# Attention scores of a Macaron layer: queries and keys split in two float32r parts instead of three bf16 parts

## The reference

```python
x = x + 0.5 * ffn(layernorm(x))      # 8 experts, top 1 by a router, 128 -> 512 -> 128
x = x + attention(layernorm(x))
x = x + 0.5 * ffn(layernorm(x))
# attention: 16 heads of DK = 8, 1024 tokens
q = (x @ Wq + bq); k = (x @ Wk + bk); v = (x @ Wv + bv)
scores = einsum('bhsd,bhtd->bhst', q, k) / sqrt(8)
ctx = einsum('bhst,bhtd->bhsd', softmax(scores), v)
return ctx @ Wo + bo
```

## Time and profile before

| what | value |
|---|---|
| time, 3 runs | 999.62 us median, 999.19 to 999.98 |
| span of the profiled execution, first to last instruction | 996.9 us |
| what lies around the span, by the median | 2.7 us |
| PE busy | 907.5 us (91%) |
| DVE busy | 832.2 us (83%) |
| ACT busy | 750.2 us (75%) |
| POOL busy | 219.1 us (22%) |
| mean granted PE clock | 0.963 of full speed |

### The profile page before, as it was taken

How to read it: one execution, slowest core, us unless ns; L and a number is a source line. 1 busy time by engine, 2 the same in 40 slices (tenths; PEclk the granted TensorE clock), 3 DMA queues, 4 the chain that set the end, 5 groups by cost and what they waited for, 6 DMA issues and landing times. The chain is left out here.

```text
span 996.9 us, 18005 instructions
## 1 busy us (share of the span) xinstructions
PE 907.5 (91%) x5949; PEld 385.6 (39%) x6023; DVE 832.2 (83%) x1404; ACT 750.2 (75%) x1507; POOL 219.1 (22%) x317
## 2 busy tenths in 40 slices
PE   5799927899999999999999999999999999965996
PEld 4699923322222222222222222222222222434996
DVE  6776628989999999999999999999999998768664
ACT  4367706978888888888888888888888888754774
POOL 3168841831000000000000100000100000024775
PEclk9989957999999999999999999999999999996998
DMA  7632135752220213202022120220202000051311
GB/s 262 194 96 73 41 116 190 238 192 63 58 61 16 62 34 81 62 17 62 15 73 74 31 62 15 73 54 28 75 30 64 29 23 17 2 169 48 105 63 44
DMA packets 65443, 75.14 MB, mean 75 GB/s; under 512 B 12896, under 2 KB 43784, under 8 KB 65352
## 3 DMA queue, kind: packets, MB, share of 16 engines
q1 hardware_dynamic: 58776, 60.98, 20.6%
q0 software_dynamic: 5120, 12.59, 4.1%
q10 hardware_dynamic: 1456, 0.41, 0.2%
HBM read 40.47 MB, written 33.49 MB: 74 GB/s over the span
## 5 line engine op out<-in xcount | busy, mean ns | idle before, releaser
L1574 DVE TENSOR_REDUCE maxima<-ps_m 128x2 f32<-128x1024 f32 x512 | 602.8, 1221 | 53.8 <-PE ps_m L1335 52.8
L1544 ACT ACTIVATE probs<-ps_s 128x512 f32<-128x512 f32 x1024 | 555.9, 600 | 109.5 <-PE ps_s L1381 77.7
L1381 PE MATMUL ps_s<-q,k 74*128 74x512 bf16 (+1 forms) x950 | 294.5, 385 | 3.0 <-ACT probs L1544 0.9
L1392 PE MATMUL ps_o<-probs,vs 128*32 128x512 f32 x2048 | 272.7, 605 | 0.7 <-ACT probs L1544 0.7
L1381 PEld LDWEIGHTS ps_s<-q,k 74*128 74x128 bf16 (+1 forms) x1024 | 79.5, 97 | 303.4 <-ACT probs L1544 217.1
L1335 PE MATMUL ps_m<-k,q 64*128 64x512 bf16 x1024 | 159.9, 385 | 13.8 <-ACT probs L1544 7.9
L1265 POOL TENSOR_SCALAR split<-top 128x16 bf16<-128x16 f32 x32 | 8.1, 253 | 445.8 <-DVE top L1590 428.7
L1335 PEld LDWEIGHTS ps_m<-k,q 64*128 64x128 bf16 x1024 | 49.1, 93 | 102.7 <-issue 58.1
L693 PE MATMUL ps_y<-W,hT 128*128 x624 | 83.8, 278 | 0.0
L1392 PEld LDWEIGHTS ps_o<-probs,vs 128*32 128x32 f32 x2048 | 40.3, 108 | 109.3 <-issue 95.1
L693 PEld LDWEIGHTS ps_y<-W,hT 128*128 128x128 f32 x624 | 77.0, 194 | 0.6 <-issue 0.4
(11 more groups left out here) (215 smaller groups left out, 586.3 us busy)
## 6 DMA issues: line engine op xcount, KB each, us to landing
k_rows<-parts SPq DMA_DIRECT2D x24, 384.0 KB, 4.5
sums<-oT SPq DMA_DIRECT2D x30, 256.0 KB, 3.6
q<-q_parts SPq DMA_DIRECT2D x75, 96.0 KB
k<-k_rows SPq DMA_DIRECT2D x15, 288.0 KB
token_rows<-x SPq DMA_DIRECT2D x16, 256.0 KB, 4.1
token_rows<-v_and_ctx SPq DMA_DIRECT2D x16, 256.0 KB, 3.6
k<-k_rows SPq DMA_DIRECT2D x15, 256.0 KB
q_parts<-parts SPq DMA_DIRECT2D x8, 384.0 KB, 3.4
```

Of the source, the lines that this page charges most:

```text
L1381: nc.tensor.matmul(ps_s[n % 3][:, :], k2[buffer(g)][0:contracted, j, kt * P:(kt + 1) * P], q2[buffer(g)][0:contracted, j, u * HALF:(u + 1) ...
L1392: last = nc.tensor.matmul(ps_o[32 * j:32 * (j + 1), :], vs[buffer(g)][:, kt, j, :], probs[:, s % 2, j, :], start=(kt == 0), stop=(kt == KT ...
L1544: nc.scalar.activation(probs[:, s % 2, j, :], ps_s[n % 3][:, :], ACT.Exp, scale=SCALE).then_inc(exped, 1)
L1574: nc.vector.tensor_reduce(maxima[:, :, pr, qt, kh], ps_m[slot][:, :, :], AX.X, ALU.max).then_inc(unit_free[slot], 1)
```

## The change

Parts are now float32r numbers, two for each value (PARTS = 2), with 2 x 2 x 8 = 32 rows of products. They, three repeated key pieces (AGAIN = 3, 24 rows, beside queries that are zero), six rows of ones beside zeros, and the two guards fill rows 0 to 63 for even heads and rows 64 to 127 for odd heads. A max unit contracts 62 rows, a score product 64, and odd and even heads lie in different halves of the rows. `second_part` and `third_part` are gone: the remainder is the second part. Stores send each part once; the load repeats it. The number of buffers of `parts` (SPLITS) goes from 3 to 2. The two max units of a step no longer stand together. The fills are whole tiles, 9 in all, and stand in the first FFN's front, before the gathers.

```diff
-PARTS = 3
+PARTS = 2
 ROWS = PARTS * PARTS * DK
-MAX_ROWS = ROWS - DK
+ODD = P // 2
 GUARDS = 2
-SCORED = ROWS + GUARDS
+AGAIN = 3
+GUARD = ODD - GUARDS
+SCORED = GUARD + GUARDS
...
-    FILLED = 4 * BUFS
+    PIECES = 3
+    FILLED = PIECES * BUFS
...
         if piece == 0:
-            self.nc.gpsimd.memset(self.k2[p][64:96, 0::2, :].bitcast(F32), self.PAIR).then_inc(self.filled, 1)
+            self.nc.gpsimd.memset(self.k2[p][:, :, :].bitcast(F32), 1.0).then_inc(self.filled, 1)
...
+        pool.wait_ge(self.normed_pool, len(self.BY_POOL))
+        for n in range(self.setup.FILLED):
+            self.setup.gpsimd_fill(pool, n)
         pool.wait_ge(self.route.stored, 2 * 16 * QUADS)
...
         for t in range(TILES):
             scatter(t)
-            if self.setup and t < self.setup.FILLED:
-                self.setup.gpsimd_fill(pool, t)
...
-SPLITS = 3
+SPLITS = 2
...
-        parts = sb("parts", [P, SPLITS, 2, PARTS, HALF], BF16)
+        parts = sb("parts", [P, SPLITS, 2, PARTS, HALF], F32)
...
-        LOADS, STORES = 2 * PARTS + 1 + 3, 1 + PARTS
+        LOADS, STORES = 2 * PARTS + 2 * PARTS * PARTS + 2 * AGAIN, 2
...
+                for n in range(PARTS):
+                    for m in range(PARTS):
+                        row = product(j, n) + m * DK
+                        engine.dma_start(k[row:row + DK, :, tokens].bitcast(F32), k_rows[n, :, :, :]).then_inc(landed, 16)
+                for n in range(AGAIN):
+                    row = j * ODD + ROWS + n * DK
+                    engine.dma_start(k[row:row + DK, :, tokens].bitcast(F32), k_rows[n % PARTS, :, :, :]).then_inc(landed, 16)
...
-                store_key(sp, QUADS - 3, 0)
                 place_guard(0)
-                store_rest(QUADS - 3)
-                for q in range(QUADS - 2, QUADS):
+                for q in range(QUADS - 3, QUADS):
                     store(q)
...
-                    for j in (2 * pr, 2 * pr + 1):
-                        rows = slice(j % 2 * MAX_ROWS, (j % 2 + 1) * MAX_ROWS)
-                        last = nc.tensor.matmul(ps_m[slot][:, j % 2, :], q2[buffer(g)][rows, j, qt * P:(qt + 1) * P],
-                                                k2[buffer(g)][rows, j, kh * HALF:(kh + 1) * HALF], start=True, stop=True)
+                    for j in range(2):
+                        rows = slice(j * ODD, j * ODD + GUARD)
+                        last = nc.tensor.matmul(ps_m[slot][:, j, :], q2[buffer(g)][rows, pr, qt * P:(qt + 1) * P],
+                                                k2[buffer(g)][rows, pr, kh * HALF:(kh + 1) * HALF], start=True, stop=True)
...
-                    nc.tensor.matmul(ps_s[n % 3][:, :], k2[buffer(g)][0:contracted, j, kt * P:(kt + 1) * P],
-                                     q2[buffer(g)][0:contracted, j, u * HALF:(u + 1) * HALF], start=True, stop=True).then_inc(scored, 1)
+                    nc.tensor.matmul(ps_s[n % 3][:, :], k2[buffer(g)][rows, j // 2, kt * P:(kt + 1) * P],
+                                     q2[buffer(g)][rows, j // 2, u * HALF:(u + 1) * HALF], start=True, stop=True).then_inc(scored, 1)
...
-                    for unit in units:
+                    for unit in units[:1]:
                         do_unit(*unit)
-                    for j in range(GH - 1):
+                    for j in range(2):
                         score(g, k, j)
+                    for unit in units[1:]:
+                        do_unit(*unit)
+                    score(g, k, 2)
                     if s:
                         values(s - 1)
                     score(g, k, GH - 1)
...
-                    nc.scalar.activation(parts[:, q % SPLITS, j, 1, :], rem[:, q % 2, j, :], ACT.Copy).then_inc(middle, 1)
...
-                for j in range(2):
-                    third_part(dve, nc.vector, LAST, j)
```

More of the change, by code:

```diff
@@ L6 @@
 BF16 = mybir.dt.bfloat16
+F32R = mybir.dt.float32r
 I32 = mybir.dt.int32
@@ L982, in attention @@
         top, negated = (sb(name, [P, 2, GH // 2 * QUAD], F32) for name in ("top", "negated"))
-        split = sb("split", [P, 2, GUARDS, GH // 2 * QUAD], BF16)
-        blocks = [sb(f"blocks{p}", [P, 4 * KT], BF16) for p in range(2)]
+        split = sb("split", [P, 2, GUARDS, GH // 2 * QUAD], F32)
+        blocks = [sb(f"blocks{p}", [P, 4 * KT], F32) for p in range(2)]
         ps_m = [ctx.enter_context(nc.psum_tensor(f"ps_m{p}", [P, 2, HALF], F32)) for p in range(2)]
@@ L1012, in use, with product @@
             return g // BUFS
-        def product(j, n, m=0):
-            row = (n * PARTS + m) * DK
-            return row if j == 0 else MAX_ROWS + row if row < MAX_ROWS else row - MAX_ROWS
-        def guard(j):
-            return ROWS if j == 0 else DK
+        def product(j, n):
+            return j % 2 * ODD + n * PARTS * DK
         def load_queries(engine, g, landed, tokens=slice(0, SEQ)):
@@ L1036, in load_keys @@
             for j in range(2):
-                k_rows = dram["k_rows"][b, :, :, :, slice(first + j, first + GH, 2), tokens].rearrange("n m d i t -> (n m d) i t")
-                many = ROWS if j == 0 else MAX_ROWS
-                engine.dma_start(k[product(j, 0):product(j, 0) + many, j::2, tokens], k_rows[0:many, :, :]).then_inc(landed, 16)
-            engine.dma_start(k[0:DK, 1::2, tokens], k_rows[MAX_ROWS:, :, :]).then_inc(landed, 16)
+                k_rows = dram["k_parts"][b, :, :, slice(first + j, first + GH, 2), tokens]
+                for n in range(PARTS):
[5 more added lines that the diff above has]
+                    engine.dma_start(k[row:row + DK, :, tokens].bitcast(F32), k_rows[n % PARTS, :, :, :]).then_inc(landed, 16)
         def high_parts(q):
@@ L1074, in stores_landed, with parts_done @@
                 engine.wait_ge(query_stored, 16 * (q + 1))
[L1076 removed]
+        def parts_done(engine, q, count):
             if q == LAST:
[L1079 removed]
+                engine.wait_ge(left[0], 2 + count)
             else:
[L1081 removed]
+                engine.wait_ge(left[min(q, FIRST)], 2 * max(q - FIRST, 0) + count)
         def landed_results(q):
@@ L1146, in place_guard @@
                     for j in range(2):
-                        sp.dma_start(q2[buffer(g)][guard(j):guard(j) + GUARDS, j::2, u * HALF:(u + 1) * HALF], rows[j, :, :, :]).then_inc(in_m[buffer(g)], 16)
+                        sp.dma_start(q2[buffer(g)][j * ODD + GUARD:j * ODD + SCORED, :, u * HALF:(u + 1) * HALF].bitcast(F32), rows[j, :, :, :]).then_inc(in_m[buffer(g)], 16)
                 def results(g, u):
@@ L1432, in _ @@
                 pe.wait_ge(high, high_parts(QUADS))
-                parts_done(pe, left, LAST, 2)
+                parts_done(pe, LAST, 2)
                 pe.wait_ge(v_out, QUADS)
@@ L1491, in high_part @@
                         nc.scalar.activation(exact[:, q % 2, j, :], bank[:, :], ACT.Identity, bias=bias[:, 0:1]).then_inc(high, 1)
-                    nc.scalar.activation(parts[:, q % SPLITS, j, 0, :], bank[:, :], ACT.Identity, bias=bias[:, 0:1]).then_inc(high, 1)
+                    nc.scalar.activation(parts[:, q % SPLITS, j, 0, :].bitcast(F32R), bank[:, :], ACT.Identity, bias=bias[:, 0:1]).then_inc(high, 1)
                 def high_both(q):
-                    parts_done(act, left, q - 2, 2)
+                    parts_done(act, q - 2, 2)
                     if q >= SPLITS:
@@ L1532, in _ @@
                         normalise(q + 2)
-                    for j in range(2):
-                        second_part(q, j)
-                parts_done(act, low, LAST - 1, 2)
-                parts_done(act, low, LAST, 2)
+                parts_done(act, LAST - 1, 2)
                 for s in range(SOFT):
@@ L1684, in remainder @@
                     dve.wait_ge(high, high_parts(q) + j + 1)
-                    nc.vector.scalar_tensor_tensor(out=rem[:, q % 2, j, :], in0=bank[:, :], scalar=bias[:, 0:1], in1=parts[:, q % SPLITS, j, 0, :],
-                                                   op0=ALU.add, op1=ALU.subtract).then_inc(left[q % LAST], 1)
+                    nc.vector.scalar_tensor_tensor(out=parts[:, q % SPLITS, j, 1, :].bitcast(F32R), in0=bank[:, :], scalar=bias[:, 0:1],
+                                                   in1=parts[:, q % SPLITS, j, 0, :], op0=ALU.add, op1=ALU.subtract).then_inc(left[q % LAST], 1)
                 front.vector(dve)
@@ L1769, in layer @@
         }
-        q2, k2 = ([sb(f"{n}{p}", [P, GH, SEQ], BF16) for p in range(BUFS)] for n in ("q2_", "k2_"))
+        q2, k2 = ([sb(f"{n}{p}", [P, GH // 2, SEQ], F32R) for p in range(BUFS)] for n in ("q2_", "k2_"))
         vs = [sb(f"vs{p}", [P, KT, GH, 32], F32) for p in range(BUFS)]
```

80 lines of the change are left out of this document (22 added, 58 removed).

## The result

The changed kernel is slower: 1065.2 us median of 4 runs (1061.18 to 1075.87) against 999.8 beside it, a ratio of 1.067 (95%: 1.063 to 1.071). The forecast was 956, the range 926 to 1002. The profiled execution has a span of 1059.1, 62.2 more than before.

A forecast was written before the change was run, and what follows sets the result against it. PE was taken to bound the loop (2.62 us a step) and POOL the first FFN's end. Against a median of 999.62, fills -10.1, step -34, last steps -1.5 and attention's start +2.5 made -43, so 956 us; range 926 to 1002.

The forecast's parts named there:

- Loop's transfers: Loop, SP's loads: 18 issues instead of 10 stay hidden; if not, 0 to 5 us in all.
- It adds 0 ... I take the bf16 end: Loop, float32r weight load behind the values, once a step: adds 0 as bf16; 0.10 (+25 us) as f32, for the range.
- the fills: First FFN, POOL: fills no longer behind the scatters, -10.1 us; at their new place they cost 0.
- one slot for a float32r product and halves that overlap: Loop, PE: float32r streams 512 columns in one slot and halves overlap, so PE needs 1.97 to 2.2 us a step.
- rivals 1 and 2: Loop, PE: float32r halves don't overlap (about 1044, chance 0.06); a float32r product streams twice or more (1045 to 1145, chance 0.08).
- the two floors of 2.40: Loop step: DVE's work and the chain through ACT's exponential each need 2.40 us, against 2.62 before.
- the allowance of 0.08: Loop step: 0.08 us added to 2.40 for unit B's wait and ACT's copy of ps_o, giving 2.48, -34 us.
- The start of attention: Before the loop: parts drop out, 2.5 us gained; waiting for quad 5's stores costs 5; net +2.5, between -4 and +7.
- Rival 3: Loop: weight load, drains between halves or unit B's wait leave a step of 2.58 to 2.63, 981 to 998; chance 0.20.
- Rival 4: Loop: PE's granted clock falls; +265 us if at 1.2 GHz throughout, +27 for a tenth of the steps; chance 0.04.
- The last 11 steps: End of the loop: scores 0 and 1 overlap in the six steps with a "y" unit, -1.5 us.

The follow-up runs named there:

- e12: The changed kernel with AGAIN = 0, so without the repeated key pieces and with 12 transfers a load: 996.71 us, ratio 0.996.
- e5: The changed kernel without copies, with bf16 parts in place of float32r and three buffers of parts: 949.18 us, ratio 0.949.
- e10: The changed kernel's layout with three bf16 parts, seven of nine products, two guards, 8 transfers a load, no copies, fills first: 948.25 us, ratio 0.946.
- e11: The kernel before with one change, its own 12 fills ahead of the gathers in the first FFN: 990.13 us, ratio 0.992.
- e8: The changed kernel without copies, with quad 5's stores issued ahead of the first guards: 991.36 us, ratio 0.991.
- e9: The changed kernel once more, nothing altered, for a comparison on one chip: 1065.61 us, ratio 1.068.
- e4: The kernel before with its 12 fills ahead of the gathers, the same kernel as e11 on another chip: 1051.91 us, ratio 0.999.
- e3: The changed kernel with 12 key transfers of each load writing 16 partitions of one head instead of 8 of two: 1181.05 us, ratio 1.122.

## Why the prediction was wrong

**The step that failed: "Loop's transfers. ... Hidden; if not, a few tenths 16 times, 0 to 5 us."** It cost 60 us in the loop, and about 4 more at the attention's start. The prediction counted how long SP issues (7 us where it was 4), and compared the guards' transpose at step 5 with their use at step 8. It named SP's wait for the results behind the load but gave it no length. They land when the load has drained: with the 18 transfers that takes 17.5 us at the place shown, with the 10 of before 8.8 (498.03 to 506.82), with e12's 12 11.7. The chain is load, results, guards, max unit, and its slack is SP's idle time before `guards<-blocks`, 4.2 us in the kernel before (3.2 to 4.4 over the groups). The earlier trace rows end where the answer begins: SP's wait behind the load, and how fast a load drains, weren't read. Most late guards were then paid twice: by PE's wait (41.4 us in all 13), and by work at the granted clock 0.50 behind it; the steps that follow the 13 waits are 12.5 us longer together than their 2.67.

**"It adds 0 ... I take the bf16 end": mis-sized.** The float32r weight load takes 185 to 193 ns, near f32's 194, and adds to the chain twice in a step, not once: at score 3 behind the values, and at score 2, which waits for ACT. The step of the kernel without copies is 2.617 on average; with bf16 it is 2.45, against 2.48 predicted. In us: first to last values 673.8 (e12) against 630.2 (e5) and 630.3 (e10), so this term is +43.5, where the bound was +25. This alone turns a gain of 40 us in the loop (35 predicted) into a loss of 3. The Trainium skill, TensorE: Matmul & The Clock Gate, section Weight-path perf modes, has fast weight load only where the weights aren't FP32. The trace bears it out if float32r counts as FP32: 185 ns in e12, 94 in bf16.

**Right: the fills** (-10.1 by e11, -10.1 predicted), on a chip where POOL ends last (in the profiles with the changed kernel's own fills x is loaded 8.1 to 10.1 us sooner); **one slot for a float32r product and halves that overlap**, so rivals 1 and 2 fell; **the two floors of 2.40**: bf16 in the same layout makes 2.39. That its average, 2.45, is so near the predicted 2.48 is in part luck: the allowance of 0.08 was for unit B's wait and ACT's copy of `ps_o`, and what fills it in e5 is PE's wait for the guards, 10.0 us, more than its 4.5 for DVE.

**The start of attention**: +4.3 against +2.5, the mechanism as predicted in part. ACT waited for quad 5's stores (3.09 us; 4.97 in e12), and putting them first is worth 5.4 us (e8). The longer wait, 5.68 us for quad 4's stores behind `load(1)`, was not foreseen, nor that the copies cost 4 us here.

**Rival 3** described the kernel without copies: a step of 2.58 to 2.63 by a slower weight load (2.617), 981 to 998 (996.7). Its upper end is not what its step gives, though: 2.63 makes 993 with the sum's other terms, and 998 only with the start's bound of +7. **Rival 4**, the clock, didn't happen by itself: in 300:850 e12's granted clock is 1.00. It fell only behind the stalls and, in some executions, after the loop (below). **The last 11 steps** were wrong in sign, +2.5 us: the "y" steps take 3.17 us (before 2.86; in bf16 halves 2.94). The float32r loads make 0.23 of it, the new layout and order 0.08.

**The end**, +3.0 us, is not the change's. Windows of the profiled execution of the changed kernel and of e9, the same kernel again, in both cases 5 to 7 us after the last values:

```profile
940.00:942.00 2.00, 1.23 (x6) 0.77 (x5) 2.00 (x8) 0.66 (x2) 2.00 (x3) 0.50 0.40 115
```

```profile
944.00:946.00 2.00, 1.42 (x13) 1.45 (x14) 2.00 (x8) 0.44 (x1) 2.00 (x3) 1.00 0.51 150
```

The same instructions run at the lower clock level in the one and at the full in the other: eight products of the output projection take 2.04 us in the one and 1.13 in e9 and in the kernel before. From the last values to the end e9 takes 120.7 us, as the kernel before. The clock falls in this way, for some 6 to 10 us, in eight of the 14 profiles and of both layouts: in e4 and not in e11, which are one kernel, and in e12 and e10 but not in e5. What decides it from one execution to the next is not known.

**The sum again**, from the changed kernel against the one before: fills and front -8.1, start +4.3 (4.1 of it the copies), step without stalls +3.2, stalls +60.3, end +3.0 (this execution's clock), together 62.7; the spans differ by 62.2.

**Open:** whether e3's pieces are worse by their source's outer dimension, as argued; what on the first chip lengthened both FFNs (in e4's trace ACT has 62.1 us of waits there that are marked "remote", and no trace from the other chips has such a row); how the drain of a load divides between bytes, number and width of its transfers.

## What to carry to other kernels

Cost a transfer not by its issue but by what lands behind it: where the issuing engine waits for a landing, as SP does here, the transfers issued ahead are in that wait, and the slack is read from the engine's idle time ahead of the next issue, not from the consumer's due time. When a format is new to a trace, ask of each weight load whether anything runs over it; here it was bare at the products that start behind a wait (0.18 us at score 2), and in the chain it counted in full. Judge a layout and a number format apart: here the layout was worth 40 us in the loop and the format took all of it back. And take a second profile of the same kernel before a difference of 3 us is put down to the change.

## What the runs showed of the hardware

- float32r: one instruction and one slot of about 0.24 us for 512 columns (520.82 and 521.06 for products that follow each other on one half of the rows, in e12), two halves of the rows at once, but a weight load of 185 ns on average for 128 columns where bf16 has 94 (e12, e5).
- The load with copies and the results behind it (1.4 and 0.26 MB) took 17.5 us to land at the place shown, at 96 GB/s and a DMA share of 0.57; the one without (1.0 MB) took 11.7. The results were waited for up to 10.6 us with copies, 8.3 without and 4.6 in the kernel before.
- A wait of 5.0 us of PE was followed by the granted clock 0.50 in the step behind it; so it was behind 11 of the 13 waits for guards, each followed by a step of 3.2 to 4.1 us. The length of the wait alone doesn't decide it: the clock had fallen after one of 1.71 us (at 400.14) and not after one of 2.00 (at 356.57).
- After the loop the granted clock fell to 0.50 for 6 to 10 us in some executions and not in others of the same kernel; it costs some 3 us.
- A fill of 128 partitions and 2048 columns takes POOL 1.80 us (e12), one of 1024 columns 0.95.
